# Head 0's row, q's low parts and the key product reordered in the attention layer; the last layer's moments on GpSimd and its rows laid out by partition

## What is computed

```python
c_adj = mean(fea, axis=1)                      # fea is x transposed, one number per node
A     = abs(abs(sigmoid(c_j - c_i) - 0.5) - 0.5) * 2
g     = relu(einsum('bcn,bnm->bcm', fea, adj * A) * para)   # q, 4 heads of 64
k, v  = split(x @ kv_w)
attn  = softmax(q k^T * scale);  out = attn v
x     = layernorm(x + out)
```

## Time and profile before

| | us |
|---|---|
| median of 3 runs | 3030.69 |
| range of the runs | 3028.7 to 3034.36 |
| the profiled execution | 3028.85 |
| its span, first to last instruction | 3026.9 |
| attention layer's batches | about 52 to 2150 |
| aggregate and output layers | about 2150 to 2905 |
| final part | about 2905 to 3027 |

### The profile page before, as it was taken

One profiled execution on the slowest core, in us unless ns is written; L12 is line 12 of the kernel. 1 busy time (PEld: TensorE's weight loads), 2 busy tenths in 40 slices (PEclk: granted clock), 3 DMA queues, 4 the chain that ended last, 5 costly groups with the idle time before them and its releaser, 6 DMA issues. The chain is left out here.

```text
span 3026.9 us, 39165 instructions
## 1 busy us (share of the span) xinstructions
PE 2815.6 (93%) x12308; PEld 1885.9 (62%) x12308; DVE 1949.0 (64%) x2917; ACT 1690.5 (56%) x2180; POOL 1218.1 (40%) x556
## 2 busy tenths in 40 slices
PE   7999999999999999999999999999599999989954
PEld 5565565656556565665656556565388888868853
DVE  5677676767767676676767767675534233338877
ACT  6566565665656666565756656564422222237768
POOL 2745546474554747446374654647300000000012
PEclk9999999999999999999999999999799999999975
DMA  4123222222222223222222322221322322305548
GB/s 132 56 68 104 76 73 63 76 71 80 95 73 69 70 69 97 80 70 73 76 70 62 107 77 64 71 63 35 112 84 98 111 83 97 111 19 184 187 161 283
DMA packets 154317, 276.19 MB, mean 91 GB/s; under 512 B 12192, under 2 KB 95136, under 8 KB 152224
## 3 DMA queue, kind: packets, MB, share of 16 engines
q1 hardware_dynamic: 154272, 275.62, 28.9%
HBM read 178.79 MB, written 62.98 MB: 80 GB/s over the span
## 5 line engine op out<-in xcount | busy, mean ns | idle before, releaser
L304 POOL TENSOR_TENSOR psum<-psum,probs 128x1024 f32<-128x1024 f32 x320 | 790.3, 2470 | 176.0 <-ACT probs L373 150.7
L373 ACT ACTIVATE probs<-sc_ps 128x1024 f32<-128x1024 f32 x512 | 504.2, 1024 | 474.3 <-PE sc_ps L831 418.1
L553 DVE TENSOR_REDUCE mx<-mx_ps 128x1 f32<-128x512 f32 x768 | 494.4, 686 | 398.6 <-PE mx_ps L796 392.8
L847 PE MATMUL pv_ps<-probs,v 128*64 128x512 f32 x2048 | 489.9, 602 | 0.0
L831 PE MATMUL sc_ps<-qb,kb 128*128 128x512 f32 x1024 | 384.2, 406 | 47.5 <-DMA qb<-row 47.5
L831 PE MATMUL sc_ps<-qa,ka 128*128 128x512 f32 x1024 | 388.3, 410 | 0.0
L796 PE MATMUL mx_ps<-ka,qa 128*128 128x512 f32 x768 | 299.5, 451 | 17.5 <-DVE mx L553 15.2
L796 PEld LDWEIGHTS mx_ps<-ka,qa 128*128 128x128 f32 x768 | 140.2, 196 | 211.8 <-DVE mx L553 135.7
L847 PEld LDWEIGHTS pv_ps<-probs,v 128*64 128x64 f32 x2048 | 129.9, 136 | 225.8 <-issue 200.6
L831 PEld LDWEIGHTS sc_ps<-qa,ka 128*128 128x128 f32 x1024 | 192.0, 192 | 111.9 <-issue 64.1
L831 PEld LDWEIGHTS sc_ps<-qb,kb 128*128 128x128 f32 x1024 | 197.6, 194 | 97.2 <-issue 47.4
(11 more groups left out here) (172 smaller groups left out, 5416.0 us busy)
## 6 DMA issues: line engine op xcount, KB each, us to landing
adj_ring<-in_adj_dram SPq DMA_DIRECT2D x128, 512.0 KB, 3.7
pre_scratch<-pre SPq DMA_DIRECT2D x28, 1024.0 KB, 4.9
pre<-pre_scratch SPq DMA_DIRECT2D x28, 1024.0 KB, 4.9
x<-in_x_dram SPq DMA_DIRECT2D x16, 1024.0 KB, 5.6
kb<-ka SPq DMA_DIRECT2D x64, 256.0 KB, 3.4
qa<-qa SPq DMA_DIRECT2D x64, 256.0 KB, 3.0
res<-in_x_dram SPq DMA_DIRECT2D x16, 1024.0 KB, 5.6
x_scratch<-res SPq DMA_DIRECT2D x16, 1024.0 KB, 4.5
```

Of the source, the lines that this page charges most:

```text
L304: pool.tensor_tensor(psum[:, h % 2, :], probs[:, 0, :] if k == 1 else psum[:, h % 2, :], probs[:, k % PR, :], ALU.add).then_inc(s["pool_ad ...
L373: nc.scalar.activation(probs[:, i % PR, :], sc_ps[:, t % 2, :], ACT.Exp, scale=SCALE)\
L553: nc.vector.tensor_reduce(mx2[:, nh, n:n + 1], mx_ps[:, nh, :], AX.X, ALU.max)\
L847: ins = nc.tensor.matmul(pv_ps[nh * HD:(nh + 1) * HD, h % 2, :], v[:, i, h * HD:(h + 1) * HD], probs[:, i % PR, nh * BANK:(nh + 1) * BANK] ...
```

## The change

In the attention layer:

- SP issues head 0's row ahead of q's copies for heads 2 and 3.
- The low parts of q are made on GpSimd for all four heads, ahead of the split of the next batch's x; DVE's instruction for head 0 is gone, and one semaphore counts all four.
- In the bubble PE makes the keys' product (`k_piece`) first and v's first half afterwards. ACT rounds q of heads 2 and 3 and the keys ahead of v's copy. DVE's two `k_low` stand among head 0's maxima, after tiles 4 and 5, and no longer among head 1's.

In the final part:

- x1 is loaded and the result stored with node `p * 8 + t` in partition p, so that a partition's piece is 8 rows, 8 KB, in one; PE's transposes read z with a step of 8 numbers for that.
- The moments' small instructions are made on GpSimd, eight for each batch, each waiting for the one before.
- ACT normalises 6 of the 8 row tiles, DVE the other 2, after the next batch's statistics. The store waits for both.
- GpSimd's groups are written out instead of looped.

```diff
@@ SP, attention
                 copy_kb(b, 1)
+                store_row(b, 0)
                 copy_qa(b, 2)
                 copy_qa(b, 3)
-                store_row(b, 0)
                 store_row(b, 1)
...
@@ GpSimd, attention
+                for h in range(HEADS):
+                    q_low(b, h)
                 if not last:
                     split_x(b + 1)
-                q_low(b, 2, last)
-                q_low(b, 3, last)
...
@@ ScalarE, attention
                 relu_q(b, 0)
+                q_high(b, 2)
+                q_high(b, 3)
+                k_high(b, 2)
+                k_high(b, 3)
+                relu_q(b, 1)
                 if not last:
-                    x_high(b + 1, range(0, 2))
+                    x_high(b + 1, range(0, 4))
                 v_copy(b, 0)
...
@@ TensorE, attention
-                v_product(b, 0, [0, 1])
+                k_piece(b, 0, 0)
+                k_piece(b, 0, 1)
                 max_scores(b, 0, 0)
                 max_scores(b, 0, 1)
-                v_product(b, 0, [2])
+                k_piece(b, 1, 0)
                 max_scores(b, 0, 2)
-                v_product(b, 0, [3])
+                k_piece(b, 1, 1)
                 max_scores(b, 0, 3)
-                for nh in range(NH):
-                    for piece in range(2):
-                        k_piece(b, nh, piece)
-                        max_scores(b, 0, 4 + 2 * nh + piece)
+                for m in range(4):
+                    v_product(b, 0, [m])
+                    max_scores(b, 0, 4 + m)
                 v_product(b, 1, [0, 1])
                 transpose_maxima(b, 0)
...
@@ final part
-    x1_v = x1.rearrange("b (t p) c -> b p t c", p=P)
-    out_v = out.rearrange("b (t p) c -> b p t c", p=P)
+    x1_v = x1.rearrange("b (p t) c -> b p t c", p=P)
+    out_v = out.rearrange("b (p t) c -> b p t c", p=P)
...
-                                                      z[:, r % 2, c, n * P:(n + 1) * P], ident[:, :])
+                                                      z[:, r % 2, c, n::T], ident[:, :])
...
+            def normalise(b, r):
+                wait(dve, s["shift_done"], b + 1)
+                for n in DVE_TILES:
+                    last = nc.vector.tensor_scalar(y[:, r, n, :], y[:, r, n, :], rstd[:, r % 2, n:n + 1],
+                                                   shift[:, r % 2, n:n + 1], ALU.mult, ALU.add)
+                last.then_inc(s["y_dve"], 1)
```

More of the change, by code:

```diff
@@ L274, in split_x, with q_low @@
                     .then_inc(s["x_split"], 1)
-            def q_low(b, h, last):
-                if h == 1:
+            def q_low(b, h):
+                if h == 0:
                     wait(pool, s["rstd_done"], 2 * b)
-                elif h == 2 and not last:
-                    wait(pool, s["x_split"], b + 2)
-                if h > 1:
-                    wait(pool, s["ql_pool"], 3 * b + h - 1)
+                else:
+                    wait(pool, s["ql_done"], 4 * b + h)
                 wait(pool, s["qr_done"], 2 * b + h // 2 + 1)
                 pool.tensor_tensor(qb[h][own(h), :], scr[own(h), h // 2, :], qa[h][own(h), :].bitcast(F32),
-                                   ALU.subtract).then_inc(s["ql_pool"], 1)
+                                   ALU.subtract).then_inc(s["ql_done"], 1)
             def body(b, last):
@@ L1513, in _, with moments @@
             pool.wait_ge(s["consts_set"], 1)
+            def moments(b, r):
+                mean_a, mean_b, sq_a, sq_b = (stats[:, r % 2, :, k] for k in (1, 4, 2, 5))
+                step = s["moment_step"]
+                wait(pool, s["shift_done"], b)
+                wait(pool, s["stats_done"], T * (b + 1))
+                pool.tensor_tensor(part[:, 0, :], mean_a, mean_b, ALU.add).then_inc(step, 1)
+                wait(pool, step, 8 * b + 1)
+                pool.tensor_tensor(part[:, 1, :], mean_a, mean_b, ALU.subtract).then_inc(step, 1)
+                wait(pool, step, 8 * b + 2)
+                pool.tensor_tensor(part[:, 2, :], sq_a, sq_b, ALU.add).then_inc(step, 1)
+                wait(pool, step, 8 * b + 3)
+                pool.tensor_scalar(neg_mean[:, :], part[:, 0, :], -0.5, None, ALU.mult).then_inc(step, 1)
+                wait(pool, step, 8 * b + 4)
+                pool.tensor_tensor(part[:, 1, :], part[:, 1, :], part[:, 1, :], ALU.mult).then_inc(step, 1)
+                wait(pool, step, 8 * b + 5)
+                pool.tensor_scalar(part[:, 2, :], part[:, 2, :], 4.0 / C, None, ALU.mult).then_inc(step, 1)
+                wait(pool, step, 8 * b + 6)
+                pool.tensor_tensor(part[:, 2, :], part[:, 2, :], part[:, 1, :], ALU.add).then_inc(step, 1)
+                wait(pool, step, 8 * b + 7)
+                pool.tensor_scalar(veps[:, :], part[:, 2, :], 0.25, EPS, ALU.mult, ALU.add).then_inc(step, 1)
             def group(g, last):
```

88 lines of the change are left out of this document (39 added, 49 removed).

## The result

| | us, median (range) | profiled span |
|---|---|---|
| before | 3029.69 (3028.58 to 3034.36) | 3026.9 |
| changed | 2953.81 (2953.09 to 2955.18) | 2953.4 |

The ratio is 0.9747, with a 95% interval of 0.973 to 0.9764: the change takes 75.9 us off, where 2962 us (67.7 us less) was predicted.

What follows compares the result with a forecast made beforehand. PE bounds attention, waiting mainly for head 0's row; in the final part the chain passes through x1 loads. 3028.85 - 64 - 5 = 2960 us for a profiled execution, given as 2962, range 2948 to 2987 (0.75).

Steps and rivals of the forecast that it cites:

- Part 1: Attention bubble: head 0's row is issued at once, so PE restarts earlier; 1.5 us per batch, 1.1 to 1.8.
- the row's way from issue to PE: Head 0's row DMA: without copies in front, 2.6 us instead of 2.92, between 2.3 and 2.92.
- GpSimd's low part of head 0 is no new wait: Attention bubble: GpSimd makes it by +6.9 us, four end near +14.9, and GpSimd is less of a bound.
- Part 2: PE's restart to v's product: without two `k_low` among head 1's maxima, 2.5 us per batch less, 1.7 to 2.9.
- Both to the end: Attention layer: both terms go through to the end, 16 x (1.5 + 2.5) = 64 us, 45 to 75.
- Part 3: Final part: 8 KB pieces, moments on GpSimd and ACT's six tiles together give -5 us, -9 to +4.
- The load: Final part: x1's load shrinks from 7.3 to about 6 us with 8 KB pieces, -1.3 over four batches.
- the rest of the round: Final part, over four batches: two batches of DVE -0.6, the moments +1.4, ACT -1.0 us.
- A: Rival, attention: the row is no earlier, only part 2 at 2.2 us is left; 2991 us, chance 0.12.
- C: Rival, attention: ACT's exponentials or GpSimd's additions set head 0's pace, no change; 3028 to 3033 us, chance 0.03.
- B: Rival, final part: stepped transposes take twice as long, 6.6 us per batch; +10 instead of -5, 2977 us, chance 0.06.
- D: Rival, final part: stepped transposes take four times 0.21 us, 13 us per batch; slower, 3069 us, chance 0.04.

Runs made afterwards that it cites:

- b_row_first: The kernel before with SP issuing head 0's row ahead of q's copies for heads 2 and 3, nothing else: 3015.52 us.
- b_row_act: b_row_first with ACT also rounding and rectifying q of heads 2 and 3 directly behind v's first copy: 2987.62 us.
- b_row_act_pool: b_row_act with GpSimd splitting the next x behind its three low parts of q, not between the first and second: 2974.69 us.
- a_split_first: The changed kernel with GpSimd's split of the next x put back behind the second of its four low parts: 2967.47 us.
- a_row_late: The changed kernel with SP's order undone, head 0's row again behind q's copies for heads 2 and 3: 2954.39 us.
- a_qlow_dve: The changed kernel with head 0's low part of q back on DVE, directly behind head 0's row: 3013.82 us.
- a_qlow_apart: a_qlow_dve with GpSimd's split of the next x waiting until DVE has made head 0's low part: 2954.28 us.
- a_klow_back: The changed kernel with DVE's two low parts of the keys back among head 1's maxima: 2979.52 us.
- the layout alone: The changed kernel with only 8 KB pieces and z read with a step; moments on DVE, ACT normalising all eight tiles: 2952.3 us.
- the moments alone: The changed kernel with moments on GpSimd and two tiles on DVE, but 1 KB pieces and z read contiguously: 2955.59 us.

## Why the prediction was right, and where it was not

**Part 1, the row: right in kind, too small, and its bound was another.** The forecast chain held: the four tiles reduced at +8.3, `k_low` directly behind them, v's first copy done at +13.6 (445.84; +13.8 forecast), the row at +16.25 (+16.3), GpSimd's low parts at +14.6 (446.78; +14.9). The term that was mis-sized is the row's way from issue to PE, taken as 2.6 and bounded below by 2.3 us. In the trace part 1 of the scores starts 2.04 us behind the issue (448.47 to 450.51) without having waited, so the row takes at most that. PE's own work ended the bubble, with a wait of 0.8 us for DVE's reductions in it; the prediction had it at +18.2 and set it aside as not binding, and it came at +18.31. The gain was 2.07 us per batch for 1.5, outside the bounds of 1.1 to 1.8. In b_row_first the restart likewise comes 2.03 us behind the issue (458.71 to 460.74), without a wait for the row.

What this part did not see is why the gain came through. It took ACT's and GpSimd's order for side matters. b_row_first shows that the restart alone leaves most of its 3 us per batch in v's second copy, b_row_act that ACT's order brings it back, b_row_act_pool and a_split_first that GpSimd's order is worth about another 1.0 us per batch. The sentence that SP "now issues the row at once" named the right effect and only one of its two sufficient causes (a_row_late).

**"GpSimd's low part of head 0 is no new wait": right, but the reason to move it was missed.** The prediction weighed DVE against GpSimd in the final part alone, where it allowed 0.4 us per batch for DVE's two tiles, and never in the bubble, where the earlier split would have met DVE's low part and cost 60 us (a_qlow_dve, a_qlow_apart). The price of leaving the instruction where it was stood nowhere in the sum, since the diff moved it. In the final part no such block shows: 31 of DVE's 32 tiles overlap an instruction of GpSimd, and all of them take about the same time.

```profile
L1576 DVE TENSOR_SCALAR pre<-pre,rstd,shift x32: 395/404/417, 2848.8 to 2946.4; 128x256 f32<-128x256 f32 x32
```

**Part 2, head 1's maxima: right.** 2.5 us were forecast. The restart to v's product went from 8.36 to 6.24 us in this batch and from 9.11 in the one of the earlier trace rows; 4.64 us per batch less part 1's 2.07 leave 2.57 us. The tile times came as counted: 6.2 us, the clock at 1.00. Of the 2.57 us 2.1 belong to the two `k_low` (a_klow_back: 8.35 us at a clock of 1.00). The other 0.4 belong to the wait that is gone: before, the stretch took 8.3 to 9.6 us, 8.8 on average, and in b_row_act, which lacks the 3 us of idling but keeps the `k_low` in their place, it takes 8.3 to 8.4 in every batch. a_klow_back costs 1.6 us per batch, net of the 0.4 that head 0's row wins.

**Both to the end:** 73.3 us against 64. The stretches between the rows of heads 1, 2 and 3, which the prediction took to be unchanged, take 21.3 and 21.7 us in both kernels.

**Part 3, the final part: the sign right, the size not.** -5 us were forecast and -0.9 measured. The round of four batches, which was to go from 27.1 to 25.6 us, did not get shorter. From DVE's addition in the fifth batch to that in the thirteenth are two such rounds: 53.7 us before (2937.68 to 2991.40), 53.7 in the changed kernel (2864.01 to 2917.66), 52.6 with the layout alone, 54.9 with the moments alone. What was gained, 1.1 us, lies ahead of the fifth batch, where nothing was forecast, and the tail loses 0.2.

Two terms failed. The load was to give 1.3 us per round; the layout alone gives about 0.55. Three of four loads take 6.4 to 6.9 us where "about 6" was written, against 6.9 to 7.4 before (once 8.1). The 415 GB/s of the earlier trace rows come from a window with nothing but loads in it, of x and of the adjacency (issued at 419.05, 419.75 and 421.39 us), at a share of 1.01; in the final part stores run beside the loads, and the DMA engines, now at 0.85, still move the 317 GB/s of before.

The other term is the rest of the round, DVE -0.6, the moments +1.4 and ACT -1.0, in all -0.2; the moments alone cost about 0.6. The moments themselves came near their count, 4.4 us with the power and the shift (2882.74 to 2887.12) for 4.1:

```profile
2882.74 0.24 POOL L1509 TENSOR_TENSOR part<-stats 128x8 f32<-128x8 f32 x1 [2.57 <-DVE stats L1590]
...
2886.92 0.20 POOL L1536 TENSOR_TENSOR shift<-neg_mean,rstd 128x8 f32<-128x8 f32 x1
```

The traces show the path to be wrong as well. The chain through the loads, as in the earlier trace rows, now goes from load to load in three batches and not in four:

```profile
2870.61 6.86 DMA pre<-x_scratch
...
2890.89 6.71 DMA pre<-x_scratch
...
2911.17 6.39 DMA pre<-x_scratch
```

A step of 20.28 us holds one load, one addition with its statistics, one set of moments, ACT's six tiles and one store's issue, and DVE's relief in a second batch does not count in it. The same step was there before, 20.33 us from the load issued at 2970.15 to the one at 2990.48. A load 0.4 to 0.5 shorter, moments 1.4 longer and ACT 1.0 shorter cancel in it. That is read from the two traces; the runs show that each half moves the round by about half a microsecond and that together they cancel, not that this step alone sets the pace.

DVE's two tiles, 0.40 us each, stand behind the next batch's addition and statistics, but the store seldom waits for them: they end behind ACT's six in 3 of the 16 batches, by 0.6 to 1.1 us.

**The sum.** 2960 was formed for a profiled execution; that of the changed kernel took 2955.18 us. Attention gave 9.3 us more than forecast, the final part 4.1 less, and 0.7 were lost between them: 4.5 us, and 2960 less 4.5 is 2955.5. So the total came close partly by luck: the shortfall of the final part covers about half of what attention gave beyond its forecast.

**The rivals.** A (2991) is out: the restart came earlier. B and D are out by one line, where PE's transposes with the 32-byte step are no slower than the contiguous ones of the earlier trace rows, 387 ns against 395:

```profile
L1606 PE MATMUL z_ps<-ident,z 128*128 128x128 f32 x256 | 51.7, 387 | 57.8 <-ACT z L1554 57.8
```

The slower reads that B and D stand for do not show in these transposes. C is out by the pace. The case that would have turned the change into little, a_qlow_dve, was not among the rivals.

## What to carry to other kernels

When the wait that ends last is taken away, list what was hidden under it on every engine that the next step needs, and price each: here the row alone gave 12 us, and ACT's and GpSimd's orders, which look like tidying, gave 41 more. Before an SBUF-only instruction of VectorE is left or put beside a long one of GpSimd, look whether the two now overlap; moving it to GpSimd or adding a wait so that the short one goes first is worth more than either engine's busy time suggests. A transfer's rate that was read where only loads ran is not its rate beside stores. When a chain closes over a ring of buffers, count each way from one load to the next, since a term that is saved in one of them may be missing in the one that binds.

## What the runs showed of the hardware

- A VectorE `scalar_tensor_tensor` of 64x1024 with both inputs in SBUF took 1.22 us alone and 4.70 us when it was issued 0.95 us into a 4.57 us `tensor_tensor` of GpSimd, ending 1.08 us behind it. VectorE's `tensor_tensor` with one input in PSUM kept 1.22 us beside GpSimd, and its 128x1024 reduction from PSUM kept 1.23 us (441.80 in the changed kernel). VectorE's `tensor_scalar` of 128x256, SBUF to SBUF, kept 0.40 us beside small instructions of GpSimd.
- The small DMA with head 0's row was usable at most 2.04 us behind its issue when no copy was queued ahead of it, and 2.92 us behind it with 0.5 MB ahead.
- PE read a stationary operand with a step of 32 bytes at the same pace as a contiguous one (387 and 395 ns per transpose).
- Small dependent instructions on GpSimd (128x8) followed each other every 0.31 us on average, the eight of the moments in 2.35 us (2882.74 to 2885.09); the same moments in seven instructions took 1.0 us on VectorE.
